# New written-out orders for the four engines of a two-layer expert and attention kernel

## What is computed

```
x = x + 0.5 * ffn(layernorm(x));  x = x + attn(layernorm(x));  x = x + 0.5 * ffn(layernorm(x))
ffn:  probs = softmax(x @ Wr)                     # 8 experts; top 2 per token, 40 slots per batch and expert
      buf[e, b, slot] = x of the tokens kept      # slot: running count of the expert's tokens in the batch
      y = relu(buf @ W1[e] + b1[e]) @ W2[e] + b2[e]   # 128 -> 512 -> 128
      out = sum over the 2 experts of y * keep * prob
attn: 16 heads, q and k of 16 features, v of 8; q = q * 16**-0.5
      A = (q . k)**2, causal over the whole batch (chunks of 64 with a carried state add up to that)
      o = (A @ v) / (sum of A + 1e-5);  out = o @ Wo
```

## Time and profile before

| | |
|---|---|
| median of three runs | 205.8 us (203.78 to 209.26) |
| the profiled execution | 204.59 us, span 202.8 us |
| TensorE busy | 185.0 us (91%) |
| TensorE weight loads busy | 145.4 us (72%) |
| ScalarE busy | 154.8 us (76%) |
| VectorE busy | 145.0 us (72%) |
| GpSimd busy | 68.5 us (34%) |
| mean granted TensorE clock | 0.983 of full |

### The profile page before, as it was taken

How to read it: one execution, slowest core, us unless ns; L and a number is a source line. 1 busy time by engine, 2 the same in 40 slices (tenths; PEclk the granted TensorE clock), 3 DMA queues, 4 the chain that set the end, 5 groups by cost and what they waited for, 6 DMA issues and landing times.

```text
span 202.8 us, 6049 instructions
## 1 busy us (share of the span) xinstructions
PE 185.0 (91%) x2329; PEld 145.4 (72%) x2329; DVE 145.0 (72%) x408; ACT 154.8 (76%) x361; POOL 68.5 (34%) x104
## 2 busy tenths in 40 slices
...
DMA packets 21741, 19.69 MB, mean 97 GB/s; under 512 B 1704, under 2 KB 18640, under 8 KB 21712
## 3 DMA queue, kind: packets, MB, share of 16 engines
...
q10 hardware_dynamic: 144, 0.00, 0.0%
...
## 4 chain that ended last, share of the span: by engine, by line
PE 76%; DVE 9%; ACT 5%; DMA 4%; issue 2%; SPq 1%; POOL 1%; DVEq 0%; ACTq 0%; POOLq 0%
PE psB L992 16%; PE psB L1062 8%; PE psS L1045 6%; PE psS L869 4%; PE psB L879 4%; PE psS L870 4%; PE psS L871 4%; PE psB L968 3%; PE psB L1064 3%; ACT amat L630 3%; DMA stack<-qk_parts 3%; DVE oh L782 2%; PE psB L928 2%; PE psB L1083 2%; PE psB L950 2%
## 5 line engine op out<-in xcount | busy, mean ns | idle before, releaser
L549 POOL TENSOR_SCALAR_AFFINE_SELECT amat<-amat 128x512 f32<-128x512 f32 x64 | 44.0, 692 | 49.1 <-ACT amat L630 48.1
L630 ACT ACTIVATE amat<-psS 128x768 f32<-128x768 f32 x64 | 49.9, 815 | 6.8 <-PE psS L1047 5.8
L601 ACT ACTIVATE hid<-psS,biasT 128x160 f32<-128x160 f32 x128 | 39.7, 401 | 10.0 <-PE psB L992 5.8
L992 PE MATMUL psB<-hid,w 128*128 128x160 f32 x256 | 40.3, 305 | 0.0
L992 PEld LDWEIGHTS psB<-hid,w 128*128 128x128 f32 x256 | 35.5, 190 | 0.7 <-DVE xTf L725 0.3
L869 PE MATMUL psS<-xe,w 128*128 128x160 f16 x128 | 27.2, 233 | 0.7 <-ACT hid L601 0.3
L870 PE MATMUL psS<-xe,w 128*128 128x160 f16 x128 | 27.2, 233 | 0.0
L871 PE MATMUL psS<-xe,w 128*128 128x160 f16 x128 | 27.2, 233 | 0.0
L1045 PE MATMUL psS<-stack 64*128 64x256 f16 x128 | 17.1, 278 | 3.7 <-ACT amat L630 2.0
L1062 PE MATMUL psB<-amat,vst 128*32 128x256 f32 x256 | 20.4, 390 | 0.0
L1045 PEld LDWEIGHTS psS<-stack 64*128 64x128 f16 x128 | 6.2, 93 | 14.0 <-issue 5.6
...
## 6 DMA issues: line engine op xcount, KB each, us to landing
...
```

The costliest lines, as they stand in the source:

```text
L549: pool.affine_select(out=d, in_=d, pattern=[[0, 2], [0, 2], [1, P]], compare_op=ALU.is_ge, fill=0.0, base=0, channel_multiplier=-1).then_i ...
L601: ins = act.activation(hid[:, n % 2, c, :], psS[:, wide_slot(s) + c // 2, (c % 2) * GS:(c % 2 + 1) * GS], ACT.Relu, bias=biasT[:, e * HC + ...
L630: act.activation(amat[:, n % A_RING, :, :], psS[:, wide_slot(s):wide_slot(s) + 2, 0:T + P], ACT.Square)\
L992: ins = mm(bank(s)[:, 0:GS], w2[:, e, c, :], hid[:, n % 2, c, :], start=(c == 0), stop=(c == HC - 1))
```

## The change

The four lists are the same sets of stages in other orders; SP's is unchanged. No instruction is added or removed. Only the places change, and with them the bank that a stage gets.

- Warm-up matmuls: 40 stand before ps.0.0 and 8 behind the first gathers, 6 between rx.0 and rx.1; before, 36 stood behind ps.0.0, and 10 and 8 among the gathers.
- In the first expert layer ups and downs alternate more; the combine of group 0 stands in one piece, ahead of up.0.1.3; pw.0.1 stands later; two more ups and one more down stand behind qk.0.
- The scores stand alone or in twos, not in threes; products of the attention stand later behind their scores and more often next to each other; oT and wo stand further apart.
- In the second expert layer the combine of group 0 stands behind the last up.
- ScalarE's and VectorE's lists follow.

```diff
 PE_STAGES = stages("""
-wc rx.0 rx.1 rl.0 rl.1 ps.0.0 warm.6.0 warm.30.1 bt dph.0.0.0 dpl.0.0.0 dph.0.0.1 warm.10.2 dpl.0.0.1
-dph.0.0.2 dpl.0.0.2 dph.0.0.3 dpl.0.0.3 warm.8.3 up.0.0.0 up.0.0.1 xt.0.2 down.0.0.0 up.0.0.2 up.0.0.3
...
-dph.0.1.3 dpl.0.1.3 pw.0.0 ot.0.0.0 ot.0.0.1 yt.0.0.0 up.0.1.0 up.0.1.1 ot.0.0.2 ot.0.0.3 down.0.1.0 up.0.1.2
-yt.0.0.1 yt.0.0.2 pw.0.1 down.0.1.1 up.0.1.3 cb.0.0.0 cb.0.0.1 up.0.1.4 cb.0.0.2 cb.0.0.3 down.0.1.2 up.0.1.5
-down.0.1.3 down.0.1.4 xt.1.0 up.0.1.6 qk.0.0.0 qk.0.0.1 qk.0.1.0 qk.0.1.1 v.0 ot.0.1.0 up.0.1.7 v.1 ot.0.1.1
-ot.0.1.2 ot.0.1.3 yt.0.1.0 down.0.1.5 down.0.1.6 xt.1.1 down.0.1.7 yt.0.1.1 yt.0.1.2 qk.1.0.0 qk.1.0.1
-qk.1.1.0 qk.1.1.1 v.2 sc.0.0 sc.0.1 cb.0.1.0 v.3 sc.0.2 cb.0.1.1 sc.0.3 cb.0.1.2 sc.0.4 cb.0.1.3 sc.0.5 av.0.0
-sc.0.6 av.0.1 sc.0.7 av.0.2 sc.1.0 sc.1.1 sc.1.2 av.0.3 sc.1.3 sc.1.4 ox.0 xt.1.2 sc.1.5 av.1.0 sc.1.6 av.1.1
-sc.1.7 oT.0 v.4 qk.2.0.0 sc.2.0 sc.2.1 qk.2.0.1 qk.2.1.0 qk.2.1.1 av.1.2 av.1.3 sc.2.2 sc.2.3 v.5 wo.0 sc.2.4
-xt.1.3 sc.2.5 av.2.0 sc.2.6 ox.1 sc.2.7 av.2.1 sc.3.0 av.2.2 sc.3.1 qk.3.0.0 sc.3.2 av.2.3 qk.3.0.1 sc.3.3
-sc.3.4 oT.1 wo.1 v.6 sc.3.5 ox.2 av.3.0 sc.3.6 av.3.1 sc.3.7 qk.3.1.0 qk.3.1.1 av.3.2 sc.4.0 oT.2 av.3.3 wo.2
-sc.4.1 sc.4.2 sc.4.3 ox.3 sc.4.4 sc.4.5 av.4.0 oT.3 sc.4.6 sc.4.7 av.4.1 wo.3 sc.5.0 av.4.2 sc.5.1 v.7 xt.2.0
-sc.5.2 av.4.3 sc.5.3 sc.5.4 ox.4 lg.1.0.0 sc.5.5 av.5.0 sc.5.6 av.5.1 sc.5.7 xt.2.1 sc.6.0 av.5.2 sc.6.1
-lg.1.0.1 oT.4 sc.6.2 sc.6.3 av.5.3 av.6.0 sc.6.4 sc.6.5 wo.4 ox.5 sc.6.6 av.6.1 sc.6.7 ps.1.0 sc.7.0 sc.7.1
-av.6.2 oT.5 sc.7.2 dph.1.0.0 av.6.3 sc.7.3 sc.7.4 av.7.0 wo.5 sc.7.5 sc.7.6 dpl.1.0.0 ox.6 dph.1.0.1 sc.7.7
-av.7.1 av.7.2 dpl.1.0.1 dph.1.0.2 dpl.1.0.2 dph.1.0.3 dpl.1.0.3 av.7.3 oT.6 up.1.0.0 wo.6 ox.7 xt.2.2 up.1.0.1
-oT.7 up.1.0.2 wo.7 up.1.0.3 down.1.0.0 down.1.0.1 pw.1.0 ot.1.0.0 lg.1.1.0 up.1.0.4 xt.2.3 down.1.0.2 lg.1.1.1
-down.1.0.3 up.1.0.5 down.1.0.4 up.1.0.6 ot.1.0.1 ps.1.1 ot.1.0.2 ot.1.0.3 up.1.0.7 down.1.0.5 dph.1.1.0
...
-ot.1.1.3 yt.1.1.0 down.1.1.6 down.1.1.7 yt.1.1.1 yt.1.1.2 yt.1.1.3 ca.1.1 cb.1.1.0 cb.1.1.1 cb.1.1.2 cb.1.1.3
+wc rx.0 warm.6.0 rx.1 rl.0 rl.1 warm.30.1 warm.10.2 ps.0.0 dph.0.0.0 dpl.0.0.0 warm.8.3 dph.0.0.1 dpl.0.0.1
+dph.0.0.2 dpl.0.0.2 dph.0.0.3 dpl.0.0.3 bt up.0.0.0 up.0.0.1 xt.0.2 down.0.0.0 up.0.0.2 down.0.0.1 up.0.0.3
...
+up.0.0.7 dph.0.1.0 dpl.0.1.0 down.0.0.6 dph.0.1.1 down.0.0.7 dpl.0.1.1 dph.0.1.2 dpl.0.1.2 pw.0.0 dph.0.1.3
+dpl.0.1.3 ot.0.0.0 ot.0.0.1 yt.0.0.0 ot.0.0.2 up.0.1.0 ot.0.0.3 yt.0.0.1 yt.0.0.2 up.0.1.1 up.0.1.2 down.0.1.0
+cb.0.0.0 cb.0.0.1 cb.0.0.2 cb.0.0.3 up.0.1.3 down.0.1.1 up.0.1.4 down.0.1.2 down.0.1.3 xt.1.0 pw.0.1 ot.0.1.0
+qk.0.0.0 qk.0.0.1 qk.0.1.0 qk.0.1.1 up.0.1.5 ot.0.1.1 ot.0.1.2 ot.0.1.3 v.0 down.0.1.4 down.0.1.5 up.0.1.6
+up.0.1.7 yt.0.1.0 v.1 down.0.1.6 down.0.1.7 xt.1.1 yt.0.1.1 yt.0.1.2 qk.1.0.0 qk.1.0.1 qk.1.1.0 qk.1.1.1
+sc.0.0 sc.0.1 cb.0.1.0 cb.0.1.1 sc.0.2 v.2 sc.0.3 sc.0.4 v.3 sc.0.5 av.0.0 av.0.1 sc.0.6 sc.0.7 cb.0.1.2
+cb.0.1.3 sc.1.0 sc.1.1 av.0.2 av.0.3 sc.1.2 sc.1.3 xt.1.2 av.1.0 sc.1.4 sc.1.5 v.4 av.1.1 sc.1.6 sc.1.7 ox.0
+qk.2.0.0 qk.2.0.1 qk.2.1.0 sc.2.0 sc.2.1 oT.0 qk.2.1.1 av.1.2 sc.2.2 sc.2.3 av.1.3 av.2.0 sc.2.4 sc.2.5 wo.0
+v.5 sc.2.6 av.2.1 sc.2.7 xt.1.3 ox.1 sc.3.0 sc.3.1 av.2.2 oT.1 sc.3.2 av.2.3 sc.3.3 sc.3.4 av.3.0 sc.3.5
+qk.3.0.0 qk.3.0.1 sc.3.6 sc.3.7 av.3.1 v.6 wo.1 ox.2 sc.4.0 sc.4.1 qk.3.1.0 qk.3.1.1 av.3.2 sc.4.2 sc.4.3 oT.2
+av.3.3 av.4.0 sc.4.4 sc.4.5 wo.2 ox.3 sc.4.6 av.4.1 sc.4.7 sc.5.0 oT.3 av.4.2 sc.5.1 wo.3 sc.5.2 v.7 sc.5.3
+av.4.3 xt.2.0 sc.5.4 sc.5.5 av.5.0 av.5.1 sc.5.6 sc.5.7 lg.1.0.0 ox.4 av.5.2 sc.6.0 xt.2.1 sc.6.1 oT.4 sc.6.2
+lg.1.0.1 sc.6.3 av.5.3 wo.4 sc.6.4 sc.6.5 av.6.0 ox.5 sc.6.6 sc.6.7 av.6.1 sc.7.0 av.6.2 sc.7.1 ps.1.0 oT.5
+sc.7.2 av.6.3 sc.7.3 sc.7.4 av.7.0 sc.7.5 wo.5 sc.7.6 av.7.1 sc.7.7 dph.1.0.0 ox.6 dpl.1.0.0 av.7.2 av.7.3
+dph.1.0.1 dpl.1.0.1 oT.6 dph.1.0.2 dpl.1.0.2 dph.1.0.3 dpl.1.0.3 wo.6 ox.7 up.1.0.0 xt.2.2 oT.7 up.1.0.1
+lg.1.1.0 wo.7 down.1.0.0 down.1.0.1 pw.1.0 up.1.0.2 up.1.0.3 ot.1.0.0 down.1.0.2 xt.2.3 up.1.0.4 lg.1.1.1
+ot.1.0.1 ot.1.0.2 ot.1.0.3 down.1.0.3 up.1.0.5 down.1.0.4 up.1.0.6 ps.1.1 down.1.0.5 up.1.0.7 dph.1.1.0
...
+cb.1.0.0 cb.1.0.1 cb.1.0.2 cb.1.0.3 down.1.1.7 yt.1.1.1 yt.1.1.2 yt.1.1.3 ca.1.1 cb.1.1.0 cb.1.1.1 cb.1.1.2
+cb.1.1.3
 """)
...
 ACT_STAGES = stages("""
...
-sc.0.3 sc.0.4 sc.0.5 ln1.1.2 sc.0.6 xe.0.0 sc.0.7 sc.1.0 sc.1.1 sc.1.2 xe.0.1 sc.1.3 sc.1.4 sc.1.5 sc.1.6
-ln1.1.3 xe.1.0 sc.1.7 qk.2.0.0 oT.0 sc.2.0 qk.2.0.1 qk.2.1.0 qk.2.1.1 sc.2.1 sc.2.2 sc.2.3 xe.1.1 sc.2.4
...
-ln1.2.0 qk.3.1.0 qk.3.1.1 oT.2 sc.4.0 xe.3.1 sc.4.1 sc.4.2 sc.4.3 sc.4.4 sc.4.5 oT.3 sc.4.6 sc.4.7 xe.4.0
...
+ln1.1.2 sc.0.5 v.2 sc.0.6 sc.0.7 v.3 sc.1.0 sc.1.1 xe.0.0 sc.1.2 sc.1.3 ln1.1.3 sc.1.4 sc.1.5 xe.0.1 xe.1.0
+sc.1.6 sc.1.7 qk.2.0.0 qk.2.0.1 qk.2.1.0 sc.2.0 sc.2.1 qk.2.1.1 sc.2.2 sc.2.3 oT.0 sc.2.4 sc.2.5 xe.1.1 sc.2.6
...
+qk.3.1.0 qk.3.1.1 ln1.2.0 sc.4.2 oT.2 sc.4.3 xe.3.1 sc.4.4 sc.4.5 sc.4.6 xe.4.0 sc.4.7 oT.3 sc.5.0 sc.5.1
+sc.5.2 sc.5.3 ln1.2.1 v.7 sc.5.4 sc.5.5 xe.4.1 xe.5.0 sc.5.6 sc.5.7 sc.6.0 sc.6.1 oT.4 sc.6.2 sc.6.3 xe.5.1
...
 """)
...
 DVE_STAGES = stages("""
...
-ot.0.0.1 pw.0.0 yt.0.0.0 sm.0.1 ot.0.0.2 ot.0.0.3 yl.0.0.0 yt.0.0.1 yt.0.0.2 yl.0.0.1 yl.0.0.2 pw.0.1 cb.0.0.0
-cb.0.0.1 ln1.1.0 cb.0.0.2 cb.0.0.3 lnx.1.0 ln2.1.0 ln1.1.1 xt.1.0 lnx.1.1 qk.0.0.0 qk.0.0.1 qk.0.1.0 qk.0.1.1
-v.0 ot.0.1.0 ot.0.1.1 ot.0.1.2 ot.0.1.3 ln2.1.1 yt.0.1.0 xt.1.1 yl.0.1.0 yt.0.1.1 yt.0.1.2 yl.0.1.1 yl.0.1.2
...
+cb.0.0.1 ln1.1.0 cb.0.0.2 cb.0.0.3 lnx.1.0 ln2.1.0 ln1.1.1 xt.1.0 ot.0.1.0 pw.0.1 qk.0.0.0 qk.0.0.1 qk.0.1.0
+qk.0.1.1 ot.0.1.1 ot.0.1.2 ot.0.1.3 lnx.1.1 v.0 yt.0.1.0 ln2.1.1 yl.0.1.0 xt.1.1 yt.0.1.1 yt.0.1.2 yl.0.1.1
+yl.0.1.2 qk.1.0.0 qk.1.0.1 qk.1.1.0 qk.1.1.1 cb.0.1.0 cb.0.1.1 ln1.1.2 lnx.1.2 cb.0.1.2 cb.0.1.3 ln2.1.2
...
 """)
```

More of the change, by code:

```diff
@@ new lines @@
+dph.0.0.2 dpl.0.0.2 dph.0.0.3 dpl.0.0.3 bt up.0.0.0 up.0.0.1 xt.0.2 down.0.0.0 up.0.0.2 down.0.0.1 up.0.0.3
+lg.0.1.0 xt.0.3 down.0.0.2 lg.0.1.1 up.0.0.4 down.0.0.3 up.0.0.5 up.0.0.6 down.0.0.4 ps.0.1 down.0.0.5
+up.0.0.7 dph.0.1.0 dpl.0.1.0 down.0.0.6 dph.0.1.1 down.0.0.7 dpl.0.1.1 dph.0.1.2 dpl.0.1.2 pw.0.0 dph.0.1.3
+dpl.0.1.3 ot.0.0.0 ot.0.0.1 yt.0.0.0 ot.0.0.2 up.0.1.0 ot.0.0.3 yt.0.0.1 yt.0.0.2 up.0.1.1 up.0.1.2 down.0.1.0
+cb.0.0.0 cb.0.0.1 cb.0.0.2 cb.0.0.3 up.0.1.3 down.0.1.1 up.0.1.4 down.0.1.2 down.0.1.3 xt.1.0 pw.0.1 ot.0.1.0
@@ new lines @@
+sc.7.2 av.6.3 sc.7.3 sc.7.4 av.7.0 sc.7.5 wo.5 sc.7.6 av.7.1 sc.7.7 dph.1.0.0 ox.6 dpl.1.0.0 av.7.2 av.7.3
+dph.1.0.1 dpl.1.0.1 oT.6 dph.1.0.2 dpl.1.0.2 dph.1.0.3 dpl.1.0.3 wo.6 ox.7 up.1.0.0 xt.2.2 oT.7 up.1.0.1
+lg.1.1.0 wo.7 down.1.0.0 down.1.0.1 pw.1.0 up.1.0.2 up.1.0.3 ot.1.0.0 down.1.0.2 xt.2.3 up.1.0.4 lg.1.1.1
+ot.1.0.1 ot.1.0.2 ot.1.0.3 down.1.0.3 up.1.0.5 down.1.0.4 up.1.0.6 ps.1.1 down.1.0.5 up.1.0.7 dph.1.1.0
+down.1.0.6 down.1.0.7 dpl.1.1.0 dph.1.1.1 dpl.1.1.1 dph.1.1.2 dpl.1.1.2 dph.1.1.3 dpl.1.1.3 yt.1.0.0 yt.1.0.1
@@ L104 @@
+up.1.1.0 up.1.1.1 yt.1.0.2 down.1.1.0 up.1.1.2 down.1.1.1 up.1.1.3 down.1.1.2 up.1.1.4 down.1.1.3 up.1.1.5
+down.1.1.4 up.1.1.6 pw.1.1 ot.1.1.0 ot.1.1.1 ot.1.1.2 down.1.1.5 ot.1.1.3 down.1.1.6 up.1.1.7 yt.1.1.0
+cb.1.0.0 cb.1.0.1 cb.1.0.2 cb.1.0.3 down.1.1.7 yt.1.1.1 yt.1.1.2 yt.1.1.3 ca.1.1 cb.1.1.0 cb.1.1.1 cb.1.1.2
+cb.1.1.3
 """)
 ACT_STAGES = stages("""
-rx.0 wr ln1.0.0 rx.1 ln1.0.1 nm.0.0 nm.0.1 w1.0 w1.1 w1.2 w1.3 dpl.0.0.0 ln1.0.2 dph.0.0.0 dph.0.0.1 bt
-dph.0.0.2 dpl.0.0.1 dph.0.0.3 dpl.0.0.2 dpl.0.0.3 up.0.0.0 w1.4 ln1.0.3 up.0.0.1 w1.5 w1.6 up.0.0.2 down.0.0.0
@@ L109 @@
[L109 to L113, removed]
@@ L124 @@
-yt.1.0.1 up.1.1.4 yt.1.0.2 down.1.1.3 down.1.1.4 up.1.1.5 up.1.1.6 down.1.1.5 up.1.1.7 yt.1.1.0 down.1.1.6
+rx.0 wr ln1.0.0 rx.1 ln1.0.1 nm.0.0 nm.0.1 w1.0 w1.1 w1.2 w1.3 ln1.0.2 dph.0.0.0 dpl.0.0.0 w1.4 dpl.0.0.1
+dph.0.0.1 dpl.0.0.2 dph.0.0.2 dpl.0.0.3 dph.0.0.3 bt up.0.0.0 w1.5 ln1.0.3 up.0.0.1 up.0.0.2 w1.6 down.0.0.0
+down.0.0.1 up.0.0.3 w1.7 down.0.0.2 up.0.0.4 down.0.0.3 up.0.0.5 ex.0.0 up.0.0.6 down.0.0.4 down.0.0.5
+up.0.0.7 dph.0.1.0 down.0.0.6 dph.0.1.1 down.0.0.7 dph.0.1.2 dph.0.1.3 ex.0.1 yt.0.0.0 up.0.1.0 yt.0.0.1
```

40 lines of the change are left out of this document (19 added, 21 removed).

## The result

The changed kernel takes 198.15 us (median of 4 runs, 197.92 to 198.41), the kernel before 205.63 on the same chip. The ratio is 0.967, 95% interval 0.963 to 0.972. The profiled execution took 198.15 us, 6.44 less than the 204.59 of before. I had forecast 200.0, and the range of 197.0 to 204.0 held it. The gain came where I had put it, with two of its terms too small; the reason that I gave for the largest one didn't survive the experiments.

What follows compares the result with a forecast made beforehand. No single limit: TensorE was nearly full in the expert layers, TensorE and ScalarE handing work to each other in the scores. Terms -1.0 - 2.4 - 1.2 - 0.3 + 0.3 = -4.6 us took 204.6 to 200.0, range 197.0 to 204.0.

Steps and rivals of the forecast that it cites:

- Neighbours: From sc.0.0 to down.1.0.0: ten fewer switches between scores, products and full-array work, 0.1 us each; -1.0 us.
- Waits of the scores and of the output products: Scores and wo stages on TensorE: waits for ScalarE go, 3.0 us, against 0.6 of new waiting; net -2.4 us.
- The four places that I named: Two runs of three scores, the run sc.6.7 to sc.7.1, and wo.1: waits of about 0.8, 0.9, 0.6, 0.7 us.
- the tight places I named: sc.0.3 to sc.0.5, sc.1.6, around sc.5.1 to sc.6.3: little work between scores; 0.6 us of new waiting.
- Operands of the first score: Before sc.0.0: more work beside the operands' trip through memory covers the 1.35 us wait; taken as -1.2 us.
- Ups and downs: First expert layer: alternating keeps TensorE and ScalarE fed, -0.6, against +0.3 at the first combine; net -0.3 us.
- The counter-term: First combine, moved earlier: TensorE arrives about 0.5 us too early for VectorE's input; +0.3 us.
- Start: Warm-up matmuls before ps.0.0, then a new gap and half clock at the gathers, mostly hidden by VectorE's one-hots; +0.3 us.
- rival B: Start: the clock stays low into the ups at about 21 us, costing 1.5 us instead of 0.3; 201.7 us, chance 0.14.
- End: Last unit: order and TensorE's 1.5 us wait before ca.1.1 both stay; 0 us, bounds -0.5 and +0.7.
- A: Scores: waits for ScalarE only change place, so the 2.4 us gain falls to 0.3; 202.5 us, chance 0.22.
- C: Attention products: wait for squares and GpSimd's masks, lead short by 0.4 us, +6.4 us; 208.8 us, chance 0.07.

Runs made afterwards that it cites:

- e5: Changed kernel with 22 of its pairs of scores pulled apart by the stage that follows, on TensorE; 202.15 us, ratio 0.988.
- e3: Kernel before with four local swaps on TensorE alone: no runs of three scores, wo.1 behind v.6 and sc.3.5; 206.27 us, ratio 1.007.
- e2: Kernel before with the new orders only from the first score to xt.2.2; 201.21 us, ratio 0.986.
- e12: Changed kernel with up.0.1.5 ahead of xt.1.0 and the first projections, on TensorE and ScalarE; 199.25 us, ratio 0.974.
- e1: Kernel before with the new orders only up to the first score, v.2 kept ahead of the scores; 202.78 us, ratio 0.995.
- e8: Changed kernel with 29 of the 32 product stages one group of scores earlier on TensorE; 218.62 us, ratio 1.070.
- e10: Changed kernel with two transposes of the gates moved into the wait before ca.1.1, VectorE's copies following; 197.64 us, ratio 0.964.
- e11: e10 with two more local moves, at oT.3 and among the first scores; 197.61 us, ratio 0.965.
- e4: Kernel before with up.0.1.6 behind the first four projections and down.0.1.4 behind xt.1.0, on TensorE alone; 204.44 us, ratio 1.000.

## Why the prediction was right, and where its sizes were off

*Neighbours (-1.0).* Right: the traces leave 0.9, and e5 gives 0.107 us per class change where nothing else changed but places. The bracket "nothing, if hidden in a wait" did not come in. The Trainium skill ("TensorEngine Tiling (Array Packing)", "Key Properties") has the drain at a change of tiling mode and no price; the price is this case's.

*Waits of the scores and of the output products (-2.4).* Waits of these kinds did go, but the term was mis-sized: -3.1 to -3.2. The four places that I named did hold 3.1 us (0.79, 0.90, 0.65 and 0.74). Four smaller ones that I had left standing went too (0.38 at sc.4.5, 0.27 at ox.4, 0.24 each at sc.6.3 and sc.7.6), 1.1 us. New waiting was 1.1 us instead of 0.6, at sc.0.4, oT.3 and av.7.1; of the tight places I named, only the first became late. The reason I gave, that the runs of three are the cause and taking them apart is the cure, was too simple: e3 did just that and gained nothing. So the term had the right sign on a reason that doesn't hold by itself, and that is luck in part. The whole new order of this stretch does gain (e2), with ScalarE's and VectorE's lists changed too; which of the lists it needs was not separated.

*Operands of the first score (-1.2).* The largest error: -2.0. I took 1.35 us from the one wait that the trace put down to the loads. By distance of starts the score was 1.42 late, v.2 before it another 0.35 (for VectorE's low part), and 0.3 more was spread. My own sums said as much: 15.7 us of work where some 13.9 stood leaves 1.8 us, not 1.35, and by the trace of before it was 13.6 (15.72 - 2.11). The 0.3 us that I held back for cb.0.1.0 did not appear: it starts 0.26 us after sc.0.1. Part of this gain, by e12, is cover for VectorE's low parts behind the first projections, which I had not seen.

*Ups and downs (-0.3).* -0.5 in the first layer. The counter-term, +0.3 for the first combine's wait for VectorE, was not seen: it starts at 48.64 with 0.23 us of lateness, as before (0.30).

*Start (+0.3).* +0.36 in the trace, and the agreement is luck: with the new start the first up begins at 21.25 to 22.17 us in seven traces (e1, e5, e8, e10, e11, e12 and the changed kernel's), with the old one at 21.00 to 21.86 in four (before, e2, e3, e4), so a single pair can't tell 0.36 from nothing. Nor had I named the last wait there, 0.94 us for the copy of the biases. The clock went as described: TensorE stood from 12.6 us, the granted clock was still 1.00 in the slice from 14, 0.70 in the next, so that it fell near 15.4, just ahead of the first gather at 15.51, then 0.50 (1.2 GHz), and it was 1.00 (2.4 GHz) again from 19. The Trainium skill's rule ("TensorE: Matmul & The Clock Gate", "What's actually happening"), that the throttled clock is the default, agrees with the drop; the work was back at full clock before the ups, so rival B's price did not fall due.

*End (0).* -0.1.

*Rivals.* A: false for this change (weight loads of scores wait 2.4 us for ScalarE, not 5), true for e3 and for the two moves of e11. B: the clock was 1.00 after 20 us. C: 1.1 us of waits for masks, not over 3; true for e8, and at a higher price than I gave it (20 us against 9 over the respective kernel).

*Observations.* All of "What would show it" came as put for "right", save one: sc.7.7 came 62.2 us after sc.0.0, just under my 62.5 to 63.5.
